# Attention and feed-forward block on one core: the attention output turned into SBUF and handled a batch at a time

## What is computed

```python
xn = layernorm(x)
q, k, v = split_heads(xn @ w_qkv)          # 16 heads of 16
scores = einsum('bqhd,bkhd->bhqk', q / 4, k)
scores = where(causal_mask, scores, -1e10)
out = einsum('bhqk,bkhd->bqhd', softmax(scores), v)
attn = out.reshape(b, s, 256) @ w_out
h = gelu(fp8(xn) @ fp8(w_gating[0])) * (fp8(xn) @ fp8(w_gating[1]))
result = x + attn + fp8(h) @ fp8(w_linear)
```

## Time and profile before

| | |
|---|---|
| median of three runs | 353.01 us (353.00 to 353.84) |
| the profiled execution | 353.47 us, of it the span of the trace 351.8 us |
| busy in the span | TensorE 336.5 us, VectorE 294.5, ScalarE 227.2, GpSimd 167.8 |
| granted TensorE clock | 0.995 of full |
| chain that ended last | TensorE 81%, VectorE 10%, ScalarE 3%, transfers 2% |

### The profile page before, as it was taken

The page is one execution under the profiler, slowest core; times in us unless marked ns, Lnnn a source line. Parts: engine busy times, 40 slices in busy tenths (PEclk is TensorE's granted clock), DMA queues, the critical chain, the costliest instruction groups (busy, mean ns, idle before and its releaser), DMA issues.

```text
span 351.8 us, 9794 instructions
## 1 busy us (share of the span) xinstructions
PE 336.5 (96%) x3514; PEld 256.8 (73%) x3514; DVE 294.5 (84%) x1359; ACT 227.2 (65%) x369; POOL 167.8 (48%) x203
## 2 busy tenths in 40 slices
PE   6899899999999999999999999999999999996996
PEld 6455456665676878788888888888888888884775
DVE  5897898888425787999999999899999999999865
ACT  1684777766655576676667766767667666775470
POOL 4214214422225364456675466664755657547461
PEclk9999999999999999999999999999999999999899
DMA  6959965673238243534528346274373552633011
GB/s 204 366 191 294 269 177 154 144 244 123 74 137 295 96 151 108 199 114 161 181 94 270 113 162 209 101 237 165 111 241 108 196 183 92 212 120 127 2 64 60
DMA packets 46569, 57.59 MB, mean 164 GB/s; under 512 B 2680, under 2 KB 39096, under 8 KB 46520
## 3 DMA queue, kind: packets, MB, share of 16 engines
q1 hardware_dynamic: 46520, 56.96, 49.9%
HBM read 16.78 MB, written 12.58 MB: 83 GB/s over the span
## 4 chain that ended last, share of the span: by engine, by line
PE 81%; DVE 10%; ACT 3%; issue 2%; DMA 2%; POOL 0%; SPq 0%; DVEq 0%; ACTq 0%; POOLq 0%
PE ps L954 13%; PE ps L845 13%; PE ps L932 11%; PE ps L905 9%; PE ps L852 7%; PE ps L832 7%; PE ps L975 6%; PE ps L809 6%; PE ps L815 6%; DVE masked L531 4%; PE ps L963 2%; PE ps L792 2%; ACT gate L618 1%; DMA xt_store<-stack 1%; DVE xn L432 1%
## 5 line engine op out<-in xcount | busy, mean ns | idle before, releaser
L531 DVE CUSTOM_DVE_ANT_0 masked<-ps,causal 128x256 bf16<-128x256 f32 (+1 forms) x512 | 148.2, 353 | 17.1 <-PE ps L905 17.1
L663 ACT ACTIVATE arena<-ps 128x1024 f32<-128x1024 f32 x96 | 98.1, 1026 | 54.7 <-PE ps L932 54.4
L366 POOL TENSOR_SCALAR_AFFINE_SELECT arena<-arena 128x512 f32<-128x512 f32 (+1 forms) x96 | 73.6, 787 | 32.9 <-ACT arena L663 32.9
L337 POOL TENSOR_TENSOR qk_part<-w_raw,qk_part 128x512 fp32r<-128x512 f32 x32 | 41.2, 1286 | 52.1 <-ACT qk_part L642 52.1
L618 ACT ACTIVATE gate<-ps 128x512 bf16<-128x512 f32 x64 | 38.6, 603 | 28.6 <-PE ps L809 28.3
L932 PE MATMUL ps<-stack 64*128 64x256 f32 (+1 forms) x512 | 51.4, 300 | 2.3 <-ACT arena L663 2.2
L845 PE MATMUL ps<-xs,wq_part 128*128 128x256 f32 x384 | 52.3, 285 | 0.3 <-ACT w_raw L636 0.3
L954 PE MATMUL ps<-arena,v_aug 128*32 128x256 f32 (+1 forms) x1024 | 49.5, 335 | 1.8 <-DVE o_norm L548 1.8
L905 PE MATMUL ps<-stack 63*128 63x256 f32 (+1 forms) x512 | 47.7, 285 | 2.0 <-DVE row_max L531 1.8
L845 PEld LDWEIGHTS ps<-xs,wq_part 128*128 128x128 f32 x384 | 47.5, 189 | 1.5 <-ACT w_raw L636 0.6
L932 PEld LDWEIGHTS ps<-stack 64*128 64x128 f32 x512 | 36.0, 186 | 15.0 <-issue 5.7
(11 more groups left out here) (64 smaller groups left out, 454.0 us busy)
## 6 DMA issues: line engine op xcount, KB each, us to landing
stack<-qk_part SPq DMA_DIRECT2D x96, 256.0 KB, 2.7
xs<-xt_store SPq DMA_DIRECT2D x16, 512.0 KB, 4.2
xt_store<-xt_part SPq DMA_DIRECT2D x14, 512.0 KB, 4.2
out_dram<-w_raw SPq DMA_DIRECT2D x15, 256.0 KB, 4.2
xres<-in_L_attn_x_dram SPq DMA_DIRECT2D x7, 512.0 KB, 6.6
arena<-in_L_ffn_w_gating_dram SPq DMA_DIRECT2D x2, 1024.0 KB, 9.3
stack<-zeros SPq DMA_DIRECT2D x4, 512.0 KB, 7.8
arena<-in_L_ffn_w_linear_dram SPq DMA_DIRECT2D x1, 1024.0 KB, 13.3
```

The lines of the kernel that those rows point to most:

```text
L337: nc.gpsimd.tensor_tensor(qk_part[:, g, QLO:KLO + 1:3, :], qk_raw[:, g, :, :], qk_part[:, g, QHI:KLO, :].bitcast(F32), ALU.subtract).then_ ...
L366: nc.gpsimd.affine_select(diag, diag, pattern=[[0, 1024 // width], [1, P]], compare_op=ALU.is_ge, fill=0.0, base=0, channel_multiplier=-1) ...
L531: last = nc.vector.tensor_tensor_reduce(masked[:, place, i * width:(i + 1) * width], max_ps[:, place, i * width:(i + 1) * width], causal[: ...
L663: nc.scalar.activation(arena[:, n, :, :], exp_banks(b, n), ACT.Exp).then_inc(exp_done, 1)
```

## The change

`o_to_rows` now turns a half out of `pv_ps` into SBUF, into `o_by_q`, which lies over the feed-forward weights `wg8` that are no longer needed; `times_v` waits for this turn (`o_by_q_done`) and no longer for the division. `o_by_q` holds both halves of a batch. For the batches 0 to 13 (`by_batch`) `normalize_o`, `round_ot` and `split_ot` then do both halves in one instruction each; the batches 14 and 15 keep one set per half. `o_norm` moves into the unused half of `xn`. In the orders, the first half's `normalize_o` in the middle of VectorE's step, its `round_ot` on ScalarE and its `split_ot` on GpSimd go; the instructions at the place of the second half do the whole batch.

```diff
@@ tensors
-        r_den = sb("r_den", [P, H], F32)
+        r_den = sb("r_den", [P, 2, 2, S // 32], F32)
+        o_by_q = wg8[:, :, :, :].rearrange("p g k n -> p (g k n)").bitcast(F32).rearrange("p (u c n) -> p u c n", u=2, c=2)
-        o_norm = sb("o_norm", [P, S], F32)
+        o_norm = xn[:, 0:2, :]
+        def by_batch(b):
+            return b < B - 2
@@ VectorE
             def o_to_rows(b, c):
                 dve.wait_ge(pv_ready, 2 * b + c + 1)
-                nc.vector.transpose(pv_bank(b, c), pv_bank(b, c)).then_inc(o_by_q_done, 1)
+                if b >= 1:
+                    dve.wait_ge(o_norm_done, 2 * b if by_batch(b - 1) else 2 * b - 1 + c)
+                nc.vector.transpose(o_by_q[:, :, c, :], pv_bank(b, c).rearrange("p (u n) -> p u n", u=2)).then_inc(o_by_q_done, 1)
             def normalize_o(b, c):
+                n = 2 if by_batch(b) else 1
+                half = slice(c, c + n)
+                done = 2 * b + c + n
...
                 if b >= 1:
                     dve.wait_ge(ot_lo, done - 2)
-                nc.vector.transpose(ot_raw[:, c, :], o_norm[:, :]).then_inc(ot_ready, 1)
+                nc.vector.transpose(ot_raw[:, half, :].rearrange("p c s -> p (c s)"),
+                                    o_norm[:, half, :].rearrange("p c s -> p (c s)")).then_inc(ot_ready, n)
@@ VectorE, step s
                     find_max(s, 1)
-                if has(s - 2):
-                    normalize_o(s - 2, 0)
...
                     find_max(s, 4)
                 if has(s - 2):
-                    normalize_o(s - 2, 1)
+                    normalize_o(s - 2, 0)
@@ ScalarE
-                act.wait_ge(ot_ready, 2 * b + c + 1)
+                n = 2 if by_batch(b) else 1
+                half = slice(c, c + n)
+                act.wait_ge(ot_ready, 2 * b + c + n)
...
-                nc.scalar.copy(ot_part[:, 0, c, :], ot_raw[:, c, :]).then_inc(ot_hi, 1)
+                nc.scalar.copy(ot_part[:, 0, half, :], ot_raw[:, half, :]).then_inc(ot_hi, n)
@@ TensorE, times_v
                 elif 2 * b + c >= 1:
-                    pe.wait_ge(o_norm_done, 2 * b + c)
+                    pe.wait_ge(o_by_q_done, 2 * b + c)
```

More of the change, by code:

```diff
@@ L369, in split_ot @@
             def split_ot(b, c):
-                pool.wait_ge(ot_hi, 2 * b + c + 1)
-                nc.gpsimd.tensor_tensor(ot_part[:, 1, c, :], ot_raw[:, c, :], ot_part[:, 0, c, :].bitcast(F32),
-                                        ALU.subtract).then_inc(ot_lo, 1)
+                n = 2 if by_batch(b) else 1
+                half = slice(c, c + n)
+                pool.wait_ge(ot_hi, 2 * b + c + n)
+                nc.gpsimd.tensor_tensor(ot_part[:, 1, half, :], ot_raw[:, half, :], ot_part[:, 0, half, :].bitcast(F32),
+                                        ALU.subtract).then_inc(ot_lo, n)
             for s in range(B):
@@ L393, in _ @@
             mask(B - 2, 5)
-            split_ot(B - 3, 1)
+            split_ot(B - 3, 0)
             for n in range(3):
@@ L539, in o_to_rows @@
                 dve.wait_ge(pv_ready, 2 * b + c + 1)
-                nc.vector.transpose(pv_bank(b, c), pv_bank(b, c)).then_inc(o_by_q_done, 1)
+                if b >= 1:
+                    dve.wait_ge(o_norm_done, 2 * b if by_batch(b - 1) else 2 * b - 1 + c)
+                nc.vector.transpose(o_by_q[:, :, c, :], pv_bank(b, c).rearrange("p (u n) -> p u n", u=2)).then_inc(o_by_q_done, 1)
             def normalize_o(b, c):
-                done = 2 * b + c + 1
-                o = pv_bank(b, c).rearrange("p (k e) -> p k e", e=2 * DH)
+                n = 2 if by_batch(b) else 1
+                half = slice(c, c + n)
+                done = 2 * b + c + n
+                o = o_by_q[:, :, half, :].rearrange("p u c (k e) -> p u (c k) e", e=2 * DH)
+                den = r_den[:, :, half, :].rearrange("p u c k -> p u (c k)")
                 dve.wait_ge(o_by_q_done, done)
-                nc.vector.reciprocal(r_den[:, :], o[:, :, DH]).then_inc(den_done, 1)
+                nc.vector.reciprocal(den, o[:, :, :, DH]).then_inc(den_done, n)
                 dve.wait_ge(den_done, done)
[L548 to L551, removed]
+                nc.vector.tensor_tensor(o_norm[:, half, :].rearrange("p c (k u d) -> p u (c k) d", u=2, d=DH), o[:, :, :, 0:DH],
+                                        den.unsqueeze(3).broadcast_to([P, 2, n * S // 32, DH]), ALU.mult).then_inc(o_norm_done, n)
                 dve.wait_ge(o_norm_done, done)
@@ L756, in _ @@
                     negate_max(s, 0)
-                if has(s - 2):
-                    round_ot(s - 2, 0)
                 if has(s - 1):
@@ L770, in _ @@
                     round_qk(s + 2, 0)
-            round_ot(B - 3, 1)
+            round_ot(B - 3, 0)
             exponent(B - 1, 0)
```

10 lines of the change are left out of this document (4 added, 6 removed).

## The result

| | before | after |
|---|---|---|
| median | 353.42 us (four runs beside it on the same chip) | 368.80 us (four runs, 366.8 to 371.21) |
| ratio | 1 | 1.040, 95% interval 1.035 to 1.046 |
| profiled execution | 353.47 us, span 351.8 | 366.80 us, span 365.0 |
| granted TensorE clock | 0.995 | 0.991 |
| eleven steady steps, from 156 us on | 157.4 us, 14.31 each | 167.1 us, eight of them 15.07 to 15.09 |

What follows compares the result with a forecast made beforehand. TensorE was taken to set the pace in the steady batches. From 353.01 us, -0.2 for a vanished wait, +1.5 for the negated maxima and +1.0 at the end gave 355.3, range 353.4 to 357.4.

Steps and rivals of the forecast that it cites:

- What bounds the kernel: Steady batches: TensorE, busy all 14.30 us, sets the pace; work taken from VectorE is worth nothing there.
- So the group takes 0.23 + 0.29 = 0.52 us longer: VectorE's combined group at the end of the step, against one half's group; bounds 0.45 and 0.6 us.
- Cost 0: Steady batches, row maxima before transpose_max: a margin of 0.84 us holds against 0.52, with 0.3 left.
- Rival D: VectorE's group longer than its rows say, transpose_max waiting in eleven batches: 1.7 us on top, 357.0; chance 0.08.
- The negated maxima, +1.5: Steady batches: split_qk and SyncE's transfers 0.77 us later, so TensorE waits before exp_scores; 1.5 us, bounds 0 to 6.9.
- half of their part: Of nine steps, one pays 0.77 us; the other eight, at 0.19 each by the median, count half: 0.75.
- The last 40 us, +1.0: Near the end, project_out(13, 0) needs both halves of batch 13 and starts 1.0 us later; bounds 0.8 to 1.2.
- Rival C, the clock: The new gap at 334 may bring a second half-clock stretch: 1.3 to 1.5 us more, 356.8; chance 0.13.
- The gain of 0.2: Steady batches: times_v waits for the turn alone, so batch 1's wait for the division goes; 0.2 us gained.
- covered by the exponentials: Last 40 us, second wait for the division, 0.35 us before 324.45: the two kernels are level within 0.1.
- a true gain: Last 40 us, third wait for the division: times_v(14, 0) starts 0.6 us sooner, given back at once.
- VectorE busy about 8 us lower: Sign in the changed kernel's trace: VectorE's busy time falls about 8 us, without effect.

Runs made afterwards that it cites:

- e1: The changed kernel, but GpSimd waits before split_qk(s+1, 1) until VectorE has done the division of batch s-2; 361.1 us.
- e7: The changed kernel, but reciprocals go into the PSUM bank, so the division has one SBUF input; times_v waits for the division again; 361.2 us.
- e5: The changed kernel with split_qk(s+1, 0) ahead of split_ot(s-3) and split_qk(s+1, 1) held until the division of batch s-2 is done; 358.0 us.
- e4: The changed kernel with all batches in halves in the old places, so only the turn into SBUF remains; 359.0 us.
- e2: The changed kernel, but on GpSimd split_qk(s+1, 0) stands ahead of split_ot(s-3); 367.6 us.
- e10: The changed kernel with reciprocals in the PSUM bank, split_qk(s+1, 0) ahead of split_ot(s-3) and batch 13 in halves, GpSimd not held; 356.0 us.
- e8: The kernel before the change, with only batches 13 to 15 turned into SBUF, in halves; 353.0 us.
- e6: The changed kernel with split_qk(s+1, 1) held until the division, split_qk(s+1, 0) ahead of split_ot(s-3), and batch 13 in halves; 355.9 us.

## Why the prediction was wrong, step by step

- **What bounds the kernel.** TensorE in the steady steps, so nothing to gain there: right. What was lost in the steps came as something reaching TensorE late; at the end a longer stretch at the lower clock came on top.
- **The step that failed: "So the group takes 0.23 + 0.29 = 0.52 us longer", hence the row maxima "Cost 0".** It took 1.44 longer. I priced the division by the addition of x, 652 ns, because both are 512 wide. But that row, and every such row I used, has one input in PSUM (`w_raw<-ps,xres`, `o_norm<-ps,r_den`). The changed division reads `o_by_q` and `r_den`, both in SBUF. The text on the change says so in plain words; I took "SBUF operands" for something that could only be a little quicker or slower. And the trace of before already had the old division beside `split_qk` (231.29 to 231.72, within 231.00 to 232.29). In the runs: 1308 ns with GpSimd at work (1.38 in the step shown), 693 with GpSimd held off (e1), 688 with one input back in PSUM (e7). In the trace this is the largest term by far: 8.5 us of the 13.2, 0.77 in each of eleven steps, 7.6 of them above the 0.08 that the width costs, and most of the 0.5 in the third.
- **The rule on two SBUF inputs.** The Trainium skill (SBUF — State Buffer, Who interferes with whom) says that a VectorE instruction with two SBUF inputs contends with a GpSimd instruction that reads SBUF. The same page of the Trainium skill (SBUF: two separate sides) says that whichever starts first has the shared ports for the whole instruction while the other blocks fully. The trace agrees: the division started at 235.94 ends 0.56 us after `split_qk` does, and then the mask behind it is the one that is late. I hadn't weighed this rule. By it, as an estimate, the division waits for `split_qk` to end, which in the rows above is 0.82 us (235.94 to 236.76). On my 0.52 that makes 1.34 of growth, 0.5 past my margin in eleven steps: 5.5 us more than the forecast, some 361.
- **Without the hold the sum was short as well.** In e5 the wide group is 0.75 longer, not 0.52: the division 0.27 (forecast 0.23), the turn back 0.27 (0.29), and the reciprocal, which I had put at "hardly more", 349 ns against about 250, with 0.1 of the spacing behind it.
- **The margin of 0.84 was 0.67.** I measured from the end of VectorE's last row maximum to TensorE's transposition as if the one could start when the other ends. Where the transposition does wait, in the changed kernel and in e5, 0.15 us lie between them. Before, it was 0.82 from here to the transposition at 234.98, so 0.67 was free:

```profile
234.07 0.09 DVE L531 DVE_READ_ACCUMULATOR2_ANT row_max<- 128x1 f32 x1
```

  That accounts for all three sizes of the group: one longer by 1.44, 0.84 (e4) or 0.75 (e5) less 0.67 gives 0.77, 0.17 and 0.08, and the steps grew by 0.77, 0.18 and 0.08. The list of waits shows only the one in front, `max_scores(s+1, 0)`, which needs the first maxima of `find_max(s, 5)`. With 0.52 the term would still have been nothing; so this error alone didn't move the forecast.
- **Rival D** had this place, at 1 us and 0.08. The place was right, the reason ("longer than its rows say") had no mechanism, and so its price was capped at 2 us over the forecast. By the margin of 0.67 its 1 us would have cost 0.33 a step.
- **The negated maxima, +1.5.** Mechanism right: the waits for them are gone as soon as `split_qk(s+1, 0)` stands in front (e2), so the bound of 0 is out. Bounds right, size too small: 2.9 us where it stands alone (e7 against e10); in the changed kernel, where it lies under the other wait, 1.2, near the 1.5 by luck. The failed part is "half of their part": six steps of e7 pay 0.1 to 1.0 us each, five pay nothing. The trace of before also had a second short wait for this transfer, 0.20 us in front of 219.63, in one of the eight steps for which I took none to be listed. The shift itself is as forecast: the stack transfers start 0.83 us later against the transposition of maxima than before (231.89 for 232.29, before 226.58 for 227.81), forecast 0.77. The delay of the maxima isn't even, since SyncE's three issues of stack transfers ahead of them take 1.87 us mostly and 2.98 at times.
- **The last 40 us, +1.0.** The new gap before `project_out(13, 0)` is there and ended by GpSimd, 1.97 us (forecast "some 1.7"), worth 1.3:

```profile
346.35 1.26 POOL L379 TENSOR_TENSOR xt_part<-xn,xt_part 128x512 fp32r<-128x512 f32 x1 [1.06 <-ACT xt_part L684]
...
347.75 0.95 PE L985 MATMUL ps<-wq_part,xt_part 128*128 128x256 f32 x6 [1.97 <-POOL xt_part L379]
```

- **Rival C, the clock.** The second stretch that I had named, behind the gap before `project_out(13, 0)`, didn't come; the first one, before it, became twice as long. The wait for the row maxima before it had grown to 1.82 and another of 0.98 followed; the thirty-two matmuls of `times_v` behind them took 2.79 us at the lower level, as those of the earlier trace rows did, and the stretch is 6.8 us long (332.4 to 339.3), against 3.4 before:

```profile
331.05 0.66 PE L915 MATMUL ps<-stack 63*128 63x128 f32 x8 [1.82 <-DVE row_max L537]
...
333.10 0.79 PE L915 MATMUL ps<-stack 63*128 63x256 f32 x4 [0.98 <-DVE row_max L537]
```

  This is in the 1.8 us that the last step is longer, for which the forecast had nothing. I didn't separate the clock from the waits in it.
- **The gain of 0.2 and the vanished waits for the division**: the waits are gone, as forecast. Which of them were worth something was partly wrong: in e8 the second, "covered by the exponentials", was worth 0.33, and the third, "a true gain", 0.03, since the row maxima take it over. The first stays in e8, so no run prices it.
- **"VectorE busy about 8 us lower"**: wrong, 2.9 higher, and that was the row that pointed to the cause.
- **What stays open.** e6 and e10 are 2.4 us and 1.9 us above before by the medians beside them. Their profiled executions are placed. e10's, 355.85 against 353.47, is longer by 0.4 ahead of the first transposition, 0.5 in the third step, 1.0 in the eleven (14.40 against 14.31, the margin of 0.67 overdrawn) and 0.6 in the last. e6's, 354.48, is 1.0 above before: 0.9 in the eleven and 0.3 in the last step, with 0.3 less ahead. The other executions have no trace. e6's go with the granted clock: 354.5 us at 0.994, 354.9 to 356.0 near 0.990, 357.4 to 358.0 near 0.985, where the kernel before took 352.6 to 355.0 near 0.994 and some 355.8 near 0.985. e10's don't sort so well. Why e6 meets the lower clock more often than the kernel before, no run shows.

## What to carry to other kernels

When an operand moves from PSUM to SBUF, ask for every reader of it on VectorE whether it now has *two* inputs in SBUF, and what GpSimd reads at that moment; price it by a row with the same places of operands, not the same width. Keeping a small operand (here the reciprocals) in PSUM is enough to avoid it; the price is the bank, for which `times_v` then waits again. Measure a margin between engines by the gap that remains where the second does wait (here 0.15 us), not down to zero. And work joined into one wide instruction comes due all at once: compare its growth with that margin of each thing queued behind it, on every engine that it passes through.

## What the runs showed of the hardware

- VectorE's float32 multiplication with both inputs in SBUF, beside a GpSimd subtraction that reads and writes SBUF: 1308 ns on average at 512 wide against 693 with GpSimd held off (e1), 1001 on average at 256 wide (e4) against 425 with one input in PSUM. In the eleven steady steps it ended 0.54 to 0.56 us after GpSimd's subtraction, and 0.29 after it at half the width (e4). Undisturbed it takes 0.69 and 0.42, both 0.13 longer than that; as an estimate from these numbers, nearly all of its elements pass after GpSimd has finished.
- It goes the other way too: GpSimd's 1024-wide mask, one of which starts during that multiplication in each step, averaged 1280 ns against 1091, and 1092 once one input was in PSUM (e7). ScalarE's rounding of 512 took 609 against 614 ns, untouched.
- A turn of 512 out of PSUM costs the same into SBUF (714 ns) as within its bank (731), and within SBUF 712. A reciprocal of 32 values takes 349 ns, of 16 about 250.
- Between the end of VectorE's last row maximum and the start of the TensorE instruction that waits for it lie 0.15 us (changed kernel and e5).
